# Sums of gathered lower rows for tiles 8 to 15 between the results of the down product

## The chip, the cores and the metric

The kernel runs on the eight cores of one Trainium2 chip, each with its own share of the rows and no traffic between them. The metric is the device time of the slowest core in microseconds, as the median of several runs.

## The reference

One layer: attention of 1024 wide rows with a causal mask, and then a mixture of eight experts with two chosen for each row, beside a shared expert. What matters here is the end of it:

```python
h = silu(einsum('nd,edf->nef', xf, w1))
ye = einsum('nef,efd->ned', h, w2)
routed = einsum('ne,ned->nd', combine, ye)          # two experts of eight for a row
shared = silu(gate) * up @ shared_down
shared = sigmoid(xf @ shared_gate_w) * shared
x = x + routed + shared
```

The output of a row is its own value after attention, plus two expert rows, each by its weight, plus the row of the shared expert by its gate.

## The kernel before

A core holds 16 tiles of 128 rows (NT = 16), each with its sum O[t] of 128 by 1024 floats in SBUF. After attention the rows are sorted by expert, 640 places for each (CAP). For each of the eight experts the loop `for ex in range(8)` computes the up product (L1089), the activation (L1096) and the down product (L1114) of five groups of 128 rows; a result is copied to one of three ys buffers, by VectorE (L1127) or, for expert 7, by ScalarE (L1124), and stored to Y in HBM by SyncE's queue (L1129).

Each row then needs two rows of Y: the lower of its two places (side 0, always of experts 0 to 6) and the higher one (side 1). `gather(t, side, ...)` has GpSimd issue one indirect DMA of 128 rows, 512 KB, for tile t into one of six buffers gb (L1150), with b = (side * NT + t) % 6. It waits until the buffer's last user is done (g_free[b]), and for the stores of Y that it needs: those up to expert 6 for side 0 (y_low), all for side 1 (y_free). `add_row` has VectorE add the gathered rows, times their weights, to O[t] (L1158), and records this as the buffer's release and as the new o_done[t].

The shared expert's down product (L1174) runs on TensorE for the 16 tiles in turn, 16 matmuls each, into two po buffers; VectorE adds each result to O[t] (L1181), which frees the po buffer and needs o_done[t]. Its weights are in SW1[0] (k_dw).

Every engine executes its own list of instructions in the order in which the program appended them, and a wait holds all that stands behind it. In the stretch in question that order is: VectorE takes the 16 adds of side 0, then for each t the result of tile t and the add of side 1 for tile t - 2. GpSimd issues the 16 gathers of side 0, then the 16 of side 1. SyncE stores a tile's output (L1187) after its second add. The adds of side 0 can begin while expert 7 is still computed.

```python
    g_free = [None] * 6
    ...
        b = (side * NT + t) % 6
```

Of the kernel before, what the change touches and what calls it, by code (L numbers as in the profile page):

```python
# [14 lines left out]
NT = 16  # L15
# [66 lines left out]
def build_program():  # L82
# [744 lines left out]
    while x < n_units or x <= max(retire_at):  # L827
        if x < n_units:
            kb, t = units[x]
# [318 lines left out]
    def gather(t, side, rows, *after):  # L1148
        b = (side * NT + t) % 6
        return b, SPOOL.dma(lambda e: e.indirect_dma_start(  # L1150
            out=gb[b][:], out_offset=None, in_=Y[0:rows, :],
            in_offset=bass.IndirectOffsetOnAxis(ap=lohi[:, side * NT + t:side * NT + t + 1], axis=0)),
            d_g[b], g_free[b], rows_out, *after)
# [3 lines left out]
    def add_row(t, side, b, k):  # L1157
        o_done[t] = SDVE.do(lambda e: e.scalar_tensor_tensor(  # L1158
            out=O[t][:], in0=gb[b][:], scalar=clh[:, side * NT + t:side * NT + t + 1], in1=O[t][:],
            op0=ALU.mult, op1=ALU.add), k, k_clh, o_done.get(t), ret[t]["xf"], o_back.get(t))  # L1160
        g_free[b] = o_done[t]

    for t in range(NT):
        b, k = gather(t, 0, 7 * CAP, *y_low, k_low, k_lohi)
        add_row(t, 0, b, k)
    SPE.wait(k_dw)
    for t in range(NT + 2):
        if t < NT:
            j = n % 2
            n += 1  # L1170
            SPE.wait(po_free[j], *[hb_ready[fc, t // 4] for fc in range(8)])
            for fc in range(8):
                for h in range(2):
                    fn = lambda e, fc=fc, h=h, j=j, t=t: e.matmul(  # L1174
                        po[j][:, h * 512:h * 512 + 512], HB[:, fc * 2048 + t * 128:fc * 2048 + t * 128 + 128],
                        SW1[0][:, fc * 1024 + h * 512:fc * 1024 + h * 512 + 512], start=(fc == 0), stop=(fc == 7))
                    if fc == 7 and h == 1:
                        k = SPE.do(fn)
                    else:
                        SPE.quiet(fn)  # L1180
            po_free[j] = o_done[t] = SDVE.do(lambda e, j=j, t=t: e.scalar_tensor_tensor(  # L1181
                out=O[t][:], in0=po[j][:], scalar=g_sb[:, t:t + 1], in1=O[t][:], op0=ALU.mult, op1=ALU.add),
                k, *cg_ready[t], o_done[t])
        if t >= 2:
            b, k = gather(t - 2, 1, 8 * CAP, *y_free)
            add_row(t - 2, 1, b, k)
            k_out = SSP.dma(lambda e, t=t - 2: e.dma_start(out=out[t * 128:(t + 1) * 128, :], in_=O[t][:]), d_outs,  # L1187
                            o_done[t - 2])
# [97 lines left out]
```

How the kernel before makes its waits and increments, by code:

```python
    def wait(self, *tokens):  # L38
        for t in tokens:
            if t is None:
                continue
            sem, val = t
            if val <= 0 or self.passed.get(id(sem), 0) >= val:
                continue
            self.passed[id(sem)] = val
            self.q.append(lambda e, s=sem, v=val: e.wait_ge(s, v))
# [1 line left out]
    def do(self, fn, *tokens):  # L48
        self.wait(*tokens)
        self.n += 1
        self.q.append(lambda e, f=fn, s=self.sem: f(e).then_inc(s, 1))
        return (self.sem, self.n)
# [5 lines left out]
    def dma(self, fn, slot, *tokens):  # L58
        self.wait(*tokens)
        slot.n += 16
        self.q.append(lambda e, f=fn, s=slot.sem: f(e).then_inc(s, 16))
        return (slot.sem, slot.n)
# [1128 lines left out]
    def run(e, main, one, other):  # L1191
        for fn in main.q:
            fn(e)
        full = e.alloc_register("full")
        e.wait_ge(*k_flag)
        e.reg_load(full, flag[0:1, 0:1])
        with e.If_eq(full, 0):
            for fn in one.q:
                fn(e)
        with e.Else():
            for fn in other.q:
                fn(e)
```

## Time and profile before

| | us |
|---|---|
| median of 3 runs | 1337.18 (1337.04 to 1341.15) |
| the profiled execution | 1337.72 |
| its span on the slowest core, 7 | 1336.2 |
| spans of the eight cores | 1319.4 to 1336.2 |
| TensorE busy, core 7 | 1145.8 (86%) |
| VectorE busy | 574.1 (43%) |
| ScalarE busy | 466.1 (35%) |
| GpSimd busy | 265.2 (20%) |

All is of one execution, taken on the slowest core unless another is named. Times in views count from the first instruction of that core. PE is TensorE, PEld its weight loads, DVE VectorE, ACT ScalarE, POOL GpSimd, SPq the queue of SyncE. A bracket behind a row of the timeline gives how long the engine stood idle before it and what released it. A row `x16` stands for several instructions merged. PEclk is the granted TensorE clock, where 1.00 is 2.4 GHz and 0.50 is 1.2 GHz. The landing of a DMA is the time from the start of its issue to its arrival.

### The profile page before, as it was taken

To read this page: it belongs to the slowest core of one execution; us is meant where nothing else is said; L and a number is where in the kernel's file an instruction comes from. 1 tells how busy PE (TensorE), PEld (TensorE's weight loads), DVE (VectorE), ACT (ScalarE), POOL (GpSimd) and SP (SyncE) were. 2 spreads that over 40 slices of the span, in tenths; PEclk is the share of its full clock that TensorE was granted. 3 is DMA by queue.
4 is the path that set the end of the run, shared out by engine and by line. 5 is a ranking of instruction groups with operands and counts; after the bars stand their busy time and mean duration, and the time that the engine had idled before them with its cause. 6 is when DMAs were issued, how large, how long until landed. Compare 5 with 4: busy or idle time off the path is not lost.

```text
span 1336.2 us, 18688 instructions; the slowest of 8 cores (1319.4 to 1336.2 us)
## 1 busy us (share of the span) xinstructions
PE 1145.8 (86%) x6280; PEld 580.3 (43%) x6280; DVE 574.1 (43%) x1273; ACT 466.1 (35%) x900; POOL 265.2 (20%) x435
## 2 busy tenths in 40 slices
PE   4678879778989898996978578699996999999887
PEld 1355445323434343442433233244563666666433
DVE  2354335335656665665674754312111111111466
ACT  2244233324543543644545443421321332222200
POOL 4101102111021112023121031360021222121431
PEclk9889889888989999998989879899998999999988
DMA  9936434997666766778959577599199999999977
GB/s 166 227 74 129 118 64 72 248 243 168 123 161 141 166 144 149 152 160 198 196 118 187 91 129 111 96 170 165 44 211 215 206 213 220 221 207 207 313 262 264
DMA packets 258828, 225.43 MB, mean 169 GB/s; under 512 B 197156, under 2 KB 203428, under 8 KB 258728
## 3 DMA queue, kind: packets, MB, share of 16 engines
q0 software_dynamic: 52848, 129.02, 45.4%
q1 hardware_dynamic: 205880, 95.14, 33.4%
q8 instruction: 54, 0.88, 0.3%
q14 instruction: 46, 0.38, 0.1%
HBM read 172.22 MB, written 51.38 MB: 167 GB/s over the span
## 4 chain that ended last, share of the span: by engine, by line
PE 53%; DMA 17%; DVE 12%; ACT 8%; issue 6%; SPq 3%; POOL 1%; DVEq 0%; ACTq 0%; POOLq 0%
PE po L605 11%; PE po L1114 8%; PE sp L1089 8%; PE sp L790 7%; PE sp L542 7%; DMA PT<-P 5%; PE po L1174 4%; PE po L484 4%; DVE per_unit L560 3%; DMA XT<-XN 3%; PE po L666 2%; DMA O<-xkv 2%; ACT P L572 2%; DMA Y<-ys 2%; DMA gb<-Y,lohi 2%
## 5 line engine op out<-in xcount | busy, mean ns | idle before, releaser
L605 PE MATMUL po<-XN,PT 128*128 128x512 bf16 x1088 | 259.3, 393 | 50.6 <-DMA PT<-P 40.8
L542 PE MATMUL sp<-XT,QT 128*128 128x512 bf16 x1088 | 255.0, 387 | 25.6 <-DMA XT<-XN 24.6
L605 PEld LDWEIGHTS po<-XN,PT 128*128 128x128 bf16 x1088 | 107.7, 101 | 193.3 <-issue 79.8
L542 PEld LDWEIGHTS sp<-XT,QT 128*128 128x128 bf16 x1088 | 106.2, 99 | 155.6 <-issue 38.2
L1127 DVE COPY ys<-po 128x1024 f32<-128x1024 f32 x35 | 42.9, 1224 | 229.8 <-PE po L1114 207.0
L790 PE MATMUL sp<-QT,WGU 128*128 128x512 bf16 x512 | 117.2, 390 | 5.9 <-DVE HB L805 5.5
L570 ACT ACTIVATE per_unit<-nm,s_q 128x1 f32<-128x1 f32 x72 | 21.2, 295 | 256.9 <-DVE nm L567 105.4
L618 DVE SCALAR_TENSOR_TENSOR O<-O,per_unit,po 128x512 f32<-128x512 f32 x112 | 80.5, 742 | 55.5 <-PE po L605 54.1
L484 PE MATMUL po<-XT,M 128*128 128x256 bf16 x512 | 65.3, 291 | 28.8 <-DMA XT<-XN 15.7
L1096 ACT ACTIVATE hT<-sp 128x640 bf16<-128x640 f32 x64 | 45.1, 704 | 113.4 <-PE sp L1089 113.4
L560 DVE TENSOR_REDUCE per_unit<-sp 128x1 f32<-128x1024 f32 (+1 forms) x72 | 83.4, 1158 | 1.6
L790 PEld LDWEIGHTS sp<-QT,WGU 128*128 128x128 bf16 x512 | 50.6, 100 | 68.8 <-issue 13.4
L572 ACT ACTIVATE P<-sp,per_unit 128x1024 bf16<-128x1024 f32 (+1 forms) x72 | 76.8, 1067 | 10.5
L69 POOL DMA_DIRECT2D xs<-xkv x60 | 32.5, 545 | 229.4 <-ACT XN L277 141.7
L666 PE MATMUL po<-WV,QT 128*128 128x512 bf16 x256 | 64.4, 397 | 10.8 <-DVE O L618 8.1
L1114 PE MATMUL po<-SW,hT 128*128 128x512 bf16 x320 | 73.2, 385 | 0.0
L1114 PE MATMUL po<-W,hT 128*128 128x512 bf16 x320 | 72.3, 379 | 0.0
L1089 PE MATMUL sp<-xt,W 128*128 128x320 bf16 x512 | 70.4, 299 | 1.5 <-ACT xt L926 1.5
L484 PEld LDWEIGHTS po<-XT,M 128*128 128x128 bf16 x512 | 52.6, 104 | 42.1 <-issue 32.0
L1089 PE MATMUL sp<-xt,SW 128*128 128x320 bf16 x512 | 70.2, 299 | 0.0
L69 POOL DMA_DIRECT2D O<-xkv x64 | 34.3, 548 | 168.4 <-ACT mvr L262 83.1
L1174 PE MATMUL po<-W,HB 128*128 128x512 bf16 x256 | 58.3, 392 | 10.6 <-DVE O L1181 10.6
(147 smaller groups left out, 1321.3 us busy)
## 6 DMA issues: line engine op xcount, KB each, us to landing
Y<-ys SPq DMA_DIRECT2D x40, 512.0 KB, 8.9
O<-xkv POOLq DMA_DIRECT2D x64, 256.0 KB, 5.7
xs<-xkv POOLq DMA_DIRECT2D x60, 256.0 KB, 3.9
G<-zero POOLq DMA_DIRECT2D x8, 1280.0 KB, 7.7
xn<-G SPq DMA_DIRECT2D x8, 1280.0 KB, 20.7
xr<-xkv POOLq DMA_DIRECT2D x16, 512.0 KB, 4.9
W<-w1p POOLq DMA_DIRECT2D x32, 256.0 KB, 16.4
W<-w2p POOLq DMA_DIRECT2D x32, 256.0 KB, 21.1
```

What stands on the lines that cost most here:

```text
L69: k = queue.dma(lambda e, i=i: e.dma_start(out=out[:, i * w:(i + 1) * w], in_=src[:, i * v:(i + 1) * v]), slot, *tokens)
L484: fn = lambda e, d1=d1, d2=d2, i=i: e.matmul(ring[i][:, 0:256], M[:, d1 * 1024 + d2 * 128:d1 * 1024 + d2 * 128 + 128], rhs(d1), start=(d1 ...
L542: fn = lambda e, d=d, h=h: e.matmul(sp[j][:, h * 512:h * 512 + 512], QT[:, d * 2048 + t * 128:d * 2048 + t * 128 + 128], XT[kb % 2][:, h * ...
L560: a = DVE.do(lambda e: e.reduce_max(lb[:, z:z + 1], sp[j][:, 0:n], axis=AX.X, negate=True), a)
L572: exp_tok[x] = ACT.do(lambda e: e.activation(out=P[p][:, 0:n], in_=sp[j][:, 0:n], func=AF.Exp, bias=ebias[:, z:z + 1], accum_out=lsum[:, z ...
L605: fn = lambda e, c=c, h=h, i=i: e.matmul(ring[i], PT[p][:, c * 128:c * 128 + 128], XN[kb % 2][:, c * 1024 + h * 512:c * 1024 + h * 512 + 5 ...
L618: ring_free[i] = DVE.do(lambda e, i=i, dst=dst: e.scalar_tensor_tensor(out=dst, in0=dst, scalar=corr[:, z:z + 1], in1=ring[i], op0=ALU.mul ...
L666: PE.quiet(lambda e, d=d, h=h, b=b: e.matmul(ring[b], QT[:, d * 2048 + t * 128:d * 2048 + t * 128 + 128], WV[:, d * 1024 + h * 512:d * 102 ...
L790: fn = lambda e, d=d, part=part: e.matmul(sp[j][:, part * 512:part * 512 + 512], WGU[fc][:, d * 256 + part * 128:d * 256 + part * 128 + 12 ...
L1089: fn = lambda e, d=d, h=h, fc=fc, i=i, j=j, xt_=xt_: e.matmul(sp[j][:, h * 512:h * 512 + H], SW1[i][:, d * 1024 + fc * 128:d * 1024 + fc * ...
L1114: fn = lambda e, fc=fc, h=h, s=s, i=i, j=j: e.matmul(po[j][:, h * 512:h * 512 + 512], hT[:, fc * CAP + s * 128:fc * CAP + s * 128 + 128], ...
L1174: fn = lambda e, fc=fc, h=h, j=j, t=t: e.matmul(po[j][:, h * 512:h * 512 + 512], HB[:, fc * 2048 + t * 128:fc * 2048 + t * 128 + 128], SW1 ...
```

## The change

The body of the first loop becomes a function `low_row(t)`, the gather of side 0 and its add. It is called for tiles 0 to 7 where the loop stood. For tiles 8 to 15 it is called in the loop of the down product, `low_row(8 + t)` ahead of the result of tile t. Both the gather on GpSimd and the add on VectorE are appended there.

```diff
--- before.py
+++ after.py
@@ -1160,11 +1160,17 @@
             op0=ALU.mult, op1=ALU.add), k, k_clh, o_done.get(t), ret[t]["xf"], o_back.get(t))
         g_free[b] = o_done[t]
 
-    for t in range(NT):
+
+    def low_row(t):
         b, k = gather(t, 0, 7 * CAP, *y_low, k_low, k_lohi)
         add_row(t, 0, b, k)
+
+    for t in range(8):
+        low_row(t)
     SPE.wait(k_dw)
     for t in range(NT + 2):
+        if 8 + t < NT:
+            low_row(8 + t)
         if t < NT:
             j = n % 2
             n += 1
```

## Rows read from the trace of the kernel before

**Rows 1.** The cores: span of each, and its mean granted TensorE clock.

```profile
core 7: 1336.2 us, clock 0.938
```

**Rows 2.** The chain of waits, core 7, 1240 to 1336 us: start, us, what.

```profile
1233.70 9.22 DMA gb<-Y,lohi
...
1243.16 1.30 DVE O L1158
...
1245.19 0.50 POOL gb L1150
...
1270.27 1.20 DVE O L1158
...
1275.24 0.14 issue
1275.38 51.29 PE po L1174 x224
```

**Rows 3.** The timeline of core 7: start, us, engine, line, operation [idle before <-releaser].

```profile
1257.67 7.07 PE L1174 MATMUL po<-W,HB 128*128 128x512 bf16 x32
...
1258.48 1.29 DVE L1158 SCALAR_TENSOR_TENSOR O<-gb,clh,O 128x1024 f32<-128x1024 f32 x1 [1.29 <-DMA gb<-Y,lohi]
...
1269.50 1.62 POOL L1150 DMA_INDIRECT gb<-Y,lohi  x1 [5.67 <-DMA Y<-ys]
...
1275.38 51.28 PE L1174 MATMUL po<-W,HB 128*128 128x512 bf16 x224 [10.64 <-DVE O L1181]
...
1281.94 1.28 DVE L1181 SCALAR_TENSOR_TENSOR O<-po,g_sb,O 128x1024 f32<-128x1024 f32 x1 [5.52 <-PE po L1174]
```

**Rows 4.** The waits of core 7, 1240 to 1336 us: us in total, times, longest.

```profile
POOL gb L1150 <- DVE O L1158: 37.7, 13, 7.9
```

**Rows 5.** Stretches of core 7: length, busy time by engine, PEclk, DMA share, GB/s.

```profile
1260.00:1265.00 5.00, 4.74 (x22) 1.96 (x20) 2.06 (x2) 0.00 (x0) 1.87 (x2) 1.00 0.96 318
...
1275.00:1282.00 7.00, 6.62 (x18) 2.49 (x19) 1.48 (x3) 0.00 (x0) 1.88 (x2) 0.57 0.97 343
1282.00:1290.00 8.00, 8.00 (x38) 3.63 (x37) 6.12 (x6) 0.00 (x0) 1.87 (x2) 1.00 0.47 151
```

**Rows 6.** Landings of gathers: core 5 all; core 7 from 1284; core 7 1255 to 1263.

```profile
DMA to landing us min/median/max: 4.7/6.7/12.8
...
DMA to landing us min/median/max: 5.8/6.6/7.1
...
L1150 POOL DMA_INDIRECT gb<-Y,lohi x5: 936/937/1686, 1253.4 to 1262.9; - x5
...
DMA to landing us min/median/max: 9.8/12.2/13.6
```

**Rows 7.** Timelines of core 3 (first three) and core 5 (last two): first lower gathers.

```profile
1218.38 1.00 POOL L1150 DMA_INDIRECT gb<-Y,lohi  x1 [22.43 <-PE sp L1089]
1219.65 0.98 POOL L1150 DMA_INDIRECT gb<-Y,lohi  x1 [0.27 <-issue]
...
1225.63 7.92 DVE L1158 SCALAR_TENSOR_TENSOR O<-gb,clh,O 128x1024 f32<-128x1024 f32 x6 [0.99 <-DMA gb<-Y,lohi]
...
1222.65 0.98 POOL L1150 DMA_INDIRECT gb<-Y,lohi  x1 [0.27 <-issue]
...
1229.07 7.58 DVE L1158 SCALAR_TENSOR_TENSOR O<-gb,clh,O 128x1024 f32<-128x1024 f32 x6 [1.50 <-DMA gb<-Y,lohi]
```

**Rows 8.** The timeline of core 0.

```profile
1237.91 2.97 PE L1114 MATMUL po<-SW,hT 128*128 128x512 bf16 x13
...
1244.93 0.70 ACT L1096 ACTIVATE hT<-sp 128x640 bf16<-128x640 f32 x1 [5.33 <-remote]
...
1245.78 17.16 PE L1114 MATMUL po<-SW,hT 128*128 128x512 bf16 x65 [4.90 <-ACT hT L1096]
...
1249.71 1.02 ACT L1124 ACTIVATE ys<-po 128x1024 f32<-128x1024 f32 x1 [4.08 <-remote]
...
1262.77 55.42 PE L1174 MATMUL po<-W,HB 128*128 128x512 bf16 x251
```

## The prediction

> **What bounds the kernel now.** First the spans of the eight cores [rows 1]: core 7 is the slowest, 1336.2 us, so its end is read first. Its chain of waits from 1240 us [rows 2] runs along gathers and VectorE adds until 1273.95 us, then on TensorE for 51.29 us without a break, and closes with VectorE's last adds. The reader is to see where TensorE entered that chain: it had begun the down product at 1257.67 us, did two tiles, and stood still until 1275.38 us [rows 3]. The second of those rows gives 10.64 us of idling, released by the VectorE step L1181. There are two po buffers, and VectorE had first to get through all 16 adds of lower rows, which were themselves waiting for gathers. After the stop the granted clock is 0.57 on average to 1282 us and then 1.00 [rows 5], that is 1.2 GHz almost to 1282 us. The first tile took from 1275.38 to its result's step at 1281.94 [rows 3], 6.5 us instead of 3.45 (16 tiles in 55.42 us on core 0 [rows 8]). So this stop costs core 7 10.6 + 3.1 = 13.7 us. Not every core has this stop: core 0 runs its 16 tiles through from 1262.77 us [rows 8]. The stop is what the change could remove. I ask what it puts there.
>
> **The change by parts.** No instruction is added or removed on any engine: still 32 gathers, 32 adds of 1.28 us, 16 results of 1.28 us, 16 stores. Eight adds move on VectorE, to before the results of down tiles 0 to 7. But the moved function also issues the gather, so eight gathers move on GpSimd too. GpSimd's order becomes: low 0 to 10, high 0, low 11, high 1, low 12, high 2, and so on to low 15, high 5, then high 6 to 15. There are six gb buffers: low t uses t mod 6, high t uses (t + 16) mod 6. Low 10 and high 0 share buffer 4; low 11 and high 1 buffer 5; 12 and 2 buffer 0; 13 and 3 buffer 1; 14 and 4 buffer 2; 15 and 5 buffer 3. These are exactly the gathers that now stand next to each other. High t can't be issued before the add of low t + 10 is over, and low t + 11 is queued behind it on GpSimd.
>
> **Start.** VectorE has low 0 to 8 behind it by about 1259.8 us (low 8's add starts at 1258.48 [rows 3]); these gathers keep their places. Tiles 0 and 1 end on TensorE at 1257.67 + 6.9 = 1264.6; the result of tile 1 goes first, low 10's add follows 1.20 us later (pitch of adds in a row [rows 2]) and ends at 1267.1. From an add's end to the issue that waits for it: 1243.16 + 1.30 to 1245.19 [rows 2], 0.75 us. So high 0 is issued at 1267.9. It also waits for expert 7's last Y store, which holds it until 1269.50 now [rows 3]; with five gathers fewer in flight I take the store to land sooner. Bounds: 0 to +1.6 us. The 10.6 us stop does vanish here: tiles 2 to 4 run to about 1275 us. Late next is GpSimd.
>
> **The loop, which is the price.** One turn, from the issue of high t to that of high t + 1: 1.27 us until low t + 11 is issued behind it (1219.65 less 1218.38 [rows 7]); that gather's landing, L; 0.24 us until VectorE starts (1233.70 + 9.22 against 1243.16 [rows 2]); the add, 1.28; 0.75 to the next issue. C = 3.5 + L. High t's own add and the down result fit into L, since high t lands earlier. For L the nearest rows are the second gathers of a burst on an idle queue: issue to add 1219.65 to 1225.63 and 1222.65 to 1229.07 us [rows 7], less 0.24, so 5.7 and 6.2 us. Below them is 4.7, the shortest landing on core 5; above them 7.1, the longest in the last stretch, where each gather runs beside a store [rows 6]. I take 6.0, as a turn too holds a store and two gathers: C = 9.5 us, between 8.2 and 10.6. TensorE needs 3.45 us a tile, or 6.5 at the low clock, so it waits in every turn. Five such turns lead from high 0 to high 5: 1267.9 + 47.5 = 1315.4 us.
>
> **After the loop.** High 5 lands and its add starts about 5.5 us after its issue (the shortest landings are 4.7 on core 5 and 5.8 in the last stretch of core 7 [rows 6], and 0.24 comes on top). The result of tile 8 stands behind it, starts 1.2 us later and takes 1.28; TensorE can then begin tile 10, 0.14 us on (as 1275.24 to 1275.38 [rows 2]): 8.1 us after the issue, at 1323.5. Tile 9 has run meanwhile, even at the low clock. Six tiles at 3.45: 1344.2. From TensorE's last matmul to the end of the span is 1336.2 - 1326.67 = 9.5 us now [rows 1, 2], and nothing in it changes: 1353.7 us. High gathers 6 to 10 follow high 5 every 1.24 us and hide under the tiles; if they didn't, their landing would cost 2 or 3 us once. For the clock after the last wait I take nothing, tile 9 having run just before; the bound is one tile's 3.1 us.
>
> **Which core.** The sum is P + 96.0, P being the start of the down product. P is 1257.67 on core 7 and 1262.77 on core 0 [rows 3, 8], so core 0 may now end last, at 1358.8. It is late because ScalarE stood twice, 5.33 and 4.08 us, on something outside the engines ("remote") while the gathers filled the queue [rows 8]. The first falls while low 0 to 10 are in flight, as they will be; the second might shrink with low 11 to 15 gone. With only the first, P is 1237.91 + 17.3 + 4.9 = 1260.1 [rows 8] and the end 1356.1. I take the slowest span as 1357. The profiled run took 1337.72 us for a span of 1336.2, and the median of the runs is 0.5 below it, so 1.0 is added: **1358 us**, 1.6% slower.
>
> The Trainium skill, "DMA: Bandwidth & Descriptors", section "Anatomy of one DMA — SWDGE (gpsimd) path", gives a GpSimd DMA about 2.0 us plus bytes over 436e3, an estimate of 3.2 us for one of these 512 KB. The trace disagrees: 4.7 us is the least [rows 6]. By that figure a turn would be bound by VectorE's two adds, the loop would lose some 14 us of its cost, and the kernel would end near 1340.
>
> **Rivals.**
> (a) Slower by the loop, as above. For it: the buffer numbers, and that GpSimd already waits 37.7 us for these adds in 13 waits [rows 4], each harmless today as its gather is wanted a few tiles later. Chance 0.78 within 1349 to 1370.
> (b) The loop, with congested landings. Between 1253 and 1263 us five gathers took 9.8 to 13.6 us [rows 6], at a DMA share of 0.96 and 318 GB/s from 1260 to 1265 us [rows 5]. At L = 9.8, C is 13.3: 1358 + 19 = 1377. Against it: a turn moves 1.5 MB in 9.5 us, some 160 GB/s. 0.07; another 0.05 for 1370 to 1375 (clock, a longer stall of ScalarE, the store's wait together).
> (c) Short landings, so that removal of the stop repays the loop. For the end at 1336.2 C must be about 6.0, L about 2.5 us; no gather read landed in under 4.7. Threshold and price are those of the loop. 0.03 for within 0.3% or near it, 0.02 for 1341 to 1349. This is where the figure of the page "DMA: Bandwidth & Descriptors" of the Trainium skill would lead.
> (d) Faster: the loop doesn't form, for instance as GpSimd's gathers stay ahead of VectorE by whole buffers. TensorE then runs 16 tiles from 1257.67, ends at 1312.9, and the kernel at 1323 (the 13.7 us back); it decides from a turn under 6.0 us on. The order of issues in the code speaks against it. 0.05.
> (e) The change does not do what it says, since low adds wait no less than before: this is a part of (a).
>
> **How the numbers follow.** Likeliest (a), 1358. Low: C = 8.5 takes off 5, core 7 alone last takes off 3: about 1350. High: C = 10.6 adds 5.5, the store's wait 1.6, the clock 3, core 0 in full 2: 1370. Range 1349 to 1370 leaves out 0.22 or less. About 0.3%, 4 us, is what a measurement of this kernel tells from no change. Slower 0.92, same 0.03, faster 0.05.
>
> **What would show it.** The order of gathers on GpSimd with single waits of several us on L1158 before high 1 to high 5, these five about 9.5 us apart; on TensorE L1174 no stop after tile 1, but one in each of tiles 5 to 9, the chain going through gb gathers and L1158; the granted clock low in that stretch; GpSimd's high 0 near 1268 us; TensorE's last matmul near 1344 us on core 7, and core 0 last or near it. The prediction is wrong if high gathers are issued without waiting for the neighbouring low add, if L is far from 6 us, or if TensorE goes through after tile 5.

## The result

The changed kernel takes 1357.83 us (median of 4 runs, 1351.7 to 1364.48), the kernel before on the same chip 1339.14 (4 runs). The ratio is 1.0139, with a 95% interval of 1.0103 to 1.0174: 1.4% slower. Some executions of every kernel here ran with a lower granted clock on the cores of one die and took longer; they are in none of the times and ratios of this document, and only the profiles of ring, ring_three, lag_three and the repeat are of such executions. The profiled execution of the changed kernel took 1351.7 us. Two of its cores, span and mean granted clock:

```profile
core 0: 1346.5 us, clock 0.936
...
core 5: 1350.1 us, clock 0.940
```

Core 5 is the slowest, so it is read. GpSimd's and VectorE's rows of its timeline (start, us, engine, line [idle before <-releaser]); L1158 is the add, L1150 the gather, L1187 the result of a down tile (L1181 before). Low t and high t are the gathers of side 0 and side 1 for tile t:

```profile
1266.03 1.28 DVE L1158 SCALAR_TENSOR_TENSOR O<-gb,clh,O 128x1024 f32<-128x1024 f32 x1
1268.23 0.94 POOL L1150 DMA_INDIRECT gb<-Y,lohi  x1 [21.16 <-DVE O L1158]
...
1269.44 0.93 POOL L1150 DMA_INDIRECT gb<-Y,lohi  x1 [0.27 <-issue]
1272.77 1.28 DVE L1158 SCALAR_TENSOR_TENSOR O<-gb,clh,O 128x1024 f32<-128x1024 f32 x1 [3.21 <-DMA gb<-Y,lohi]
...
1274.62 1.28 DVE L1158 SCALAR_TENSOR_TENSOR O<-gb,clh,O 128x1024 f32<-128x1024 f32 x1 [0.56 <-DMA gb<-Y,lohi]
1275.82 1.28 DVE L1187 SCALAR_TENSOR_TENSOR O<-po,g_sb,O 128x1024 f32<-128x1024 f32 x1
1276.97 0.94 POOL L1150 DMA_INDIRECT gb<-Y,lohi  x1 [6.60 <-issue]
...
1278.18 0.94 POOL L1150 DMA_INDIRECT gb<-Y,lohi  x1 [0.27 <-issue]
1281.36 1.28 DVE L1158 SCALAR_TENSOR_TENSOR O<-gb,clh,O 128x1024 f32<-128x1024 f32 x1 [4.26 <-DMA gb<-Y,lohi]
1283.42 1.28 DVE L1158 SCALAR_TENSOR_TENSOR O<-gb,clh,O 128x1024 f32<-128x1024 f32 x1 [0.77 <-DMA gb<-Y,lohi]
...
1285.45 0.94 POOL L1150 DMA_INDIRECT gb<-Y,lohi  x1 [6.33 <-DVE O L1158]
```

This is one turn and its beginning. Low 10's add (1266.03) ends at 1267.3, high 0 is issued at 1268.23, low 11 behind it at 1269.44. High 0's add runs at 1272.77, low 11's at 1274.62, and then high 1 can be issued: 1276.97. The next turn ends at 1285.45. In the kernel before, GpSimd waits at this place for a store [rows 3]. TensorE's rows of the same core:

```profile
1257.58 17.43 PE L1180 MATMUL po<-W,HB 128*128 128x512 bf16 x80
1277.25 3.61 PE L1180 MATMUL po<-W,HB 128*128 128x512 bf16 x16 [2.24 <-DVE O L1187]
1286.04 5.23 PE L1180 MATMUL po<-W,HB 128*128 128x512 bf16 x16 [5.18 <-DVE O L1187]
1294.42 3.61 PE L1180 MATMUL po<-W,HB 128*128 128x512 bf16 x16 [3.15 <-DVE O L1187]
1303.02 5.27 PE L1180 MATMUL po<-W,HB 128*128 128x512 bf16 x16 [4.99 <-DVE O L1187]
1312.03 5.30 PE L1180 MATMUL po<-W,HB 128*128 128x512 bf16 x16 [3.73 <-DVE O L1187]
1318.52 3.61 PE L1180 MATMUL po<-W,HB 128*128 128x512 bf16 x16 [1.19 <-DVE O L1187]
1322.59 17.43 PE L1180 MATMUL po<-W,HB 128*128 128x512 bf16 x80 [0.46 <-DVE O L1187]
```

The one stop of 10.64 us after tile 1 [rows 3] is gone, and there are six others, in front of tiles 5 to 10: 2.24 + 5.18 + 3.15 + 4.99 + 3.73 + 1.19, with a last one of 0.46 in front of tile 11: 20.9 us. The waits of core 5, 1255 to 1350 us (total, times, longest):

```profile
POOL gb L1150 <- DVE O L1158: 51.8, 8, 21.2
...
DVE O L1158 <- DMA gb<-Y,lohi: 29.3, 10, 5.3
PE po L1180 <- DVE O L1187: 20.9, 7, 5.2
```

And its chain of waits in the same stretch (start, us, what), with one landing for each turn:

```profile
1269.44 5.09 DMA gb<-Y,lohi
...
1274.62 1.30 DVE O L1158
...
1276.97 0.94 POOL gb L1150
...
1278.18 5.14 DMA gb<-Y,lohi
...
1286.66 5.04 DMA gb<-Y,lohi
...
1293.83 5.21 DMA gb<-Y,lohi
...
1302.43 5.61 DMA gb<-Y,lohi
...
1312.64 7.16 DMA gb<-Y,lohi
...
1322.59 17.44 PE po L1180 x80
```

GpSimd's 37.7 us of waits for adds [rows 4] have become 51.8, and now they lie in the chain: a gather, an add, GpSimd, the next gather. In three stretches (length, then busy time of TensorE, its weight loads, VectorE, ScalarE and GpSimd with their instructions, then PEclk, DMA share and GB/s):

```profile
1257.60:1275.00 17.40, 17.40 (x81) 7.70 (x79) 7.90 (x7) 1.02 (x1) 1.87 (x2) 1.00 0.27 94
1275.00:1318.50 43.50, 23.04 (x81) 8.64 (x81) 19.46 (x16) 0.00 (x0) 13.20 (x14) 0.88 0.56 186
1318.50:1340.00 21.50, 21.02 (x96) 9.24 (x96) 15.97 (x13) 0.00 (x0) 5.38 (x6) 1.00 1.01 367
```

In the middle one, 43.5 us, TensorE is busy for 23, VectorE for 19.5, GpSimd for 13 and the DMA engines for 56%. No engine fills it; what it waits for is each time the next issue.

**A measure that scatters less.** The start of the down product, P, lies between 1228 and 1258 us on the eight cores of this one execution. Most of that spread is older than the stretch in question: the last up matmul (L1089) ends between 1211 and 1238 us. So I read each core's span less its own P. "P less up" is the time from the end of the last up matmul to P. The granted clock from P to the last matmul was 0.85 to 1.00 on every core of every profile here, but for pool_only further down, where it was 0.78 or 0.79.

| profiled execution | span less P, eight cores | latest P | P less up |
|---|---|---|---|
| before | 65.0, 65.2, 72.7, 65.0, 75.4, 72.5, 77.8, 78.5 | 1262.8 | 24.9, 27.9, 17.1, 31.8, 17.1, 17.1, 17.1, 17.1 |
| after | 93.3, 95.0, 93.2, 94.0, 93.1, 92.5, 94.6, 92.5 | 1257.6 | 17.1 but for 19.2 (core 5) and 25.5 (core 7) |

The stretch became 14 to 30 us longer, but the kernel only 19. One reason is that the slowest core before, 7, had the longest stretch, 78.5, and lost the least. The other is in the last column: the cores that had 65 us and no stop of TensorE, 0, 1 and 3, are the three that came late to P, 25 to 32 us after the last up matmul instead of 17. While they were late their lower rows were added (all 16 adds are over by P), so the stop was saved at the price of a delay of 8 to 15 us. Counted from the end of the last up matmul (the two columns added), the kernel before takes 89.6 to 96.8 us, 92.8 at the median of the cores, and the changed one 110.2 to 118.0, 111.4 at the median: 18.6 us more, which is what the kernel lost.

### The profile page after: what moved, and what is told of

Same layout as the page of the kernel before. It is cut to its first block, busy times and chain, and to the rows that moved or that the text cites. A ratio compares the mean times of both kernels' runs of the same rounds, so it can differ in the third digit from the quotient of the medians.

```text
span 1350.1 us, 18678 instructions; the slowest of 8 cores (1323.2 to 1350.1 us)
## 1 busy us (share of the span) xinstructions
PE 1146.2 (85%) x6280; PEld 580.6 (43%) x6280; DVE 574.2 (43%) x1273; ACT 465.9 (35%) x900; POOL 264.1 (20%) x435
## 4 chain that ended last, share of the span: by engine, by line
PE 57%; DMA 17%; DVE 11%; ACT 6%; issue 5%; SPq 3%; POOL 0%; DVEq 0%; ACTq 0%; POOLq 0%
PE po L605 12%; PE po L1114 9%; PE sp L1089 9%; PE sp L542 8%; PE sp L790 7%; DMA PT<-P 5%; PE po L484 4%; PE po L666 3%; DMA XT<-XN 3%; DMA gb<-Y,lohi 2%; DVE per_unit L560 2%; DMA O<-xkv 2%; ACT P L572 2%; PE po L1180 2%; DMA Y<-ys 2%
## 5 line engine op out<-in xcount | busy, mean ns | idle before, releaser
L542 PE MATMUL sp<-XT,QT 128*128 128x512 bf16 x1088 | 252.2, 385 | 22.3 <-DMA XT<-XN 21.2
L570 ACT ACTIVATE per_unit<-nm,s_q 128x1 f32<-128x1 f32 x72 | 21.2, 295 | 257.7 <-DVE nm L567 101.4
L484 PE MATMUL po<-XT,M 128*128 128x256 bf16 x512 | 69.0, 302 | 32.6 <-DMA XT<-XN 19.5
L1096 ACT ACTIVATE hT<-sp 128x640 bf16<-128x640 f32 x64 | 44.9, 704 | 117.6 <-PE sp L1089 110.5
L1180 PE MATMUL po<-W,HB 128*128 128x512 bf16 x256 | 61.5, 402 | 20.9 <-DVE O L1187 20.9
L1089 PE MATMUL sp<-xt,W 128*128 128x320 bf16 x512 | 70.4, 299 | 1.5 <-ACT xt L926 1.5
L1089 PE MATMUL sp<-xt,SW 128*128 128x320 bf16 x512 | 70.2, 299 | 0.0
## 6 DMA issues: line engine op xcount, KB each, us to landing
W<-w1p POOLq DMA_DIRECT2D x32, 256.0 KB, 15.7
```

The lines of the kernel that those rows point to most:

```text
L484: fn = lambda e, d1=d1, d2=d2, i=i: e.matmul(ring[i][:, 0:256], M[:, d1 * 1024 + d2 * 128:d1 * 1024 + d2 * 128 + 128], rhs(d1), start=(d1 ...
L542: fn = lambda e, d=d, h=h: e.matmul(sp[j][:, h * 512:h * 512 + 512], QT[:, d * 2048 + t * 128:d * 2048 + t * 128 + 128], XT[kb % 2][:, h * ...
L1089: fn = lambda e, d=d, h=h, fc=fc, i=i, j=j, xt_=xt_: e.matmul(sp[j][:, h * 512:h * 512 + H], SW1[i][:, d * 1024 + fc * 128:d * 1024 + fc * ...
L1180: fn = lambda e, fc=fc, h=h, j=j, t=t: e.matmul(po[j][:, h * 512:h * 512 + 512], HB[:, fc * 2048 + t * 128:fc * 2048 + t * 128 + 128], SW1 ...
```

## The experiments

### VectorE's sequence alone, and GpSimd's alone

```diff
-        return b, SPOOL.dma(lambda e: e.indirect_dma_start(
+        (last if side else first).append(lambda: SPOOL.dma(lambda e: e.indirect_dma_start(
...
+    for issue in first + last:
+        issue()
```

The adds stay where the change puts them, the 16 lower gathers are issued first.

> One half of the change alone: VectorE's sequence as changed, but GpSimd issues all 16 lower gathers first, as in the kernel before. Queue theory (the loop forms because low t + 11 stands behind high t on GpSimd): the five turns vanish, the span less the start of the down product (P) falls from 92.5 to 95 us to about 66, and the median to 1323 to 1330 us. Buffer theory (high t and low t + 10 share a buffer, and VectorE's new order adds low t + 10 only just before high t is wanted): the turns stay, now of 0.75 (issue after the add) + about 4.8 (landing of a lone gather) + 0.24 + 1.2 (high's add) + 1.28 (next low add) = 8.3 us, between 8.0 and 8.8, so the median stays between 1350 and 1360 us.

Measured: ratio 1.0173 (1.0062 to 1.0283, from two executions); span less P 88.6 to 92.2 us on the eight cores. Core 0:

```profile
1257.93 0.94 POOL L1153 DMA_INDIRECT gb<-Y,lohi  x1 [2.70 <-DVE O L1162]
...
1262.52 2.48 DVE L1162 SCALAR_TENSOR_TENSOR O<-gb,clh,O 128x1024 f32<-128x1024 f32 x2 [3.26 <-DMA gb<-Y,lohi]
...
1265.75 0.94 POOL L1153 DMA_INDIRECT gb<-Y,lohi  x1 [6.88 <-DVE O L1162]
...
1271.10 2.48 DVE L1162 SCALAR_TENSOR_TENSOR O<-gb,clh,O 128x1024 f32<-128x1024 f32 x2 [4.91 <-DMA gb<-Y,lohi]
...
1274.33 0.94 POOL L1153 DMA_INDIRECT gb<-Y,lohi  x1 [7.65 <-DVE O L1162]
...
1281.81 0.94 POOL L1153 DMA_INDIRECT gb<-Y,lohi  x1 [6.55 <-DVE O L1162]
```

The lower gathers are all issued before the first high one (the last at 1254.29), and the turns are there all the same: 7.82, 8.58 and 7.48 us from one high gather to the next. High's add and the next low add now follow each other at once (x2), and the low one frees the buffer of the next high gather. The queue theory falls: at the median of the eight cores the stretch is only 3 us shorter than with the whole change (90.5 against 93.3). In the chain of this core these gathers, with no second one behind them, land in 4.09 to 5.19 us, against 5.04 to 5.61 in the changed kernel: a difference of the size of those 3 us.

The other half, with VectorE's 16 adds first:

```diff
-    for t in range(8):
+    for t in range(NT):
         low_row(t)
...
+    for issue in first[:11] + [f for i in range(5) for f in (last[i], first[11 + i])] + last[5:]:
+        issue()
```

> The other half alone: GpSimd's sequence as changed, VectorE's as in the kernel before. Both theories agree on a turn here: low 11 to 15 each wait behind a high gather that waits for the low add before it, 1.24 + about 5.2 + 0.24 + 1.28 + 0.75 = 8.7 us, five times, and nothing of the down product's results can be taken meanwhile: TensorE stops after tile 1 for about 40 us and the time is 1365 to 1378 us. If instead GpSimd's order costs nothing by itself, the time is that of the kernel before, 1337 to 1341.

Measured: 1377.57 us (one execution; the kernel before took 1344.2 there), span less P 108.3 to 111.2. Core 3, two of the turns and TensorE after them:

```profile
1281.45 0.94 POOL L1153 DMA_INDIRECT gb<-Y,lohi  x1 [6.69 <-issue]
1282.65 0.93 POOL L1153 DMA_INDIRECT gb<-Y,lohi  x1 [0.27 <-issue]
1287.90 1.28 DVE L1162 SCALAR_TENSOR_TENSOR O<-gb,clh,O 128x1024 f32<-128x1024 f32 x1 [7.52 <-DMA gb<-Y,lohi]
1289.94 0.94 POOL L1153 DMA_INDIRECT gb<-Y,lohi  x1 [6.35 <-DVE O L1162]
...
1315.72 14.57 PE L1182 MATMUL po<-W,HB 128*128 128x512 bf16 x56 [40.93 <-DVE O L1189]
```

A turn of 8.49 us, five of them in front of all results, and TensorE stops once, for 40.93 us. So each half makes the loop by itself, and the halves don't add: in the changed kernel they share the same round trip, and at the median of the cores the stretch is 93.3 us, beside 90.5 for VectorE's half and 109.6 for GpSimd's.

### The buffer numbers

```diff
-        b = (side * NT + t) % 6
+        b = gn[0] % 6
+        gn[0] += 1
```

> The changed kernel with the buffer of a gather numbered by the order of issue (a ring of six) in place of (16 * side + t) mod 6; the order on both engines is that of the change. Buffer theory: a gather waits for the add six places back, the turns vanish, TensorE has no stop but perhaps 1 to 3 us near tile 4 while high 0 waits for the last Y store; span less P 65 to 70 us, median 1322 to 1332, below the kernel before by about 1%. Rival, VectorE's load (three steps of 1.25 us a tile while low adds last, against 3.45 for TensorE): the turns shrink only to 3.75 and the gain is the same within 2 us, so this run can't tell a small load from none, but it would show any other cause by a stop of TensorE that stays at 8 us a tile and a median above 1350.

Measured: span less P 66.1 to 73.5 us. On core 5 TensorE runs its 16 tiles in 55.6 us without a stop:

```profile
1261.57 55.64 PE L1182 MATMUL po<-W,HB 128*128 128x512 bf16 x256
```

Both orders are those of the change; only the numbers differ, and 24 us of the stretch are gone at the median of the cores (69.5). This shows the buffer theory. The other seven cores kept stops, of 0.4 to 6.4 us in all. On core 7 they are 4.02, 0.34 and 1.10 us, and the gathers come late there: the add that starts at 1283.75 us is of a gather (low 12) issued at 1272.28, some 11 us earlier, in a stretch with a DMA share of 0.99. These are the long landings of rival (b), which the loop had kept away.

The time is another matter: ratio 0.9966 (0.9915 to 1.0017), a median of 1340.9 against 1344.2 on that chip. I had expected 1322 to 1332, and this failed. There was less to win than the 13.7 us of core 7: without its stop, core 0 with the latest P would have ended last, at 1327.8 in place of 1336.2. And counted from the last up matmul the ring takes 88.6 us at the median of the cores, only 4 less than the kernel before.

### One number changed: how many rows come first

```diff
-    for t in range(8):
+    for t in range(10):
...
-        if 8 + t < NT:
-            low_row(8 + t)
+        if 10 + t < NT:
+            low_row(10 + t)
```

> The changed kernel with one number changed: ten lower rows come ahead of the down product, not eight, so low t + 10 is added two tiles before high t is. Buffer numbers unchanged. Buffer theory: a gather needs about 0.75 + 5 + 0.24 + 1.28 = 7.3 us from the add that frees its buffer to the end of its own, which two tiles (6.9 us) and the slack of the two po buffers nearly cover: no turn over 3.8 us, span less P 66 to 70 us on cores whose gathers are early, a stop of 1 to 3 us after tile 1 on those whose are late; median 1322 to 1332. Queue theory expects the same order of size. If the loop came from neither (for instance from gathers and output stores sharing the DMA engines), about half of it would stay and the median would be above 1340.

> The changed kernel with nine lower rows ahead of the down product in place of eight. Buffer theory: low t + 10 is added one tile before high t is wanted, so a round trip (0.75 + about 5 + 0.24 + 1.28 for high t's add + 1.28 for the low add behind it = 8.5 us) is spread over two tiles: turns of 4.3 us against TensorE's 3.45, five of them; span less P about 70 us (69 to 73), between the 66.3 to 71.0 of ten ahead and the 92.5 to 95.0 of eight, and much nearer the former. A theory in which a turn's cost shrinks evenly with each row moved would give about 81.

Measured: with ten, span less P 66.3 to 71.0 us; with nine, 71.0 to 74.0. Two executions with ten took 1336.33 and 1343.44 us (the kernel before 1344.2 there; 1322 to 1332 was expected and not reached), one with nine 1338.0 (1337.3). On core 0 with nine:

```profile
1280.47 3.61 PE L1180 MATMUL po<-W,HB 128*128 128x512 bf16 x16 [0.30 <-DVE O L1187]
1287.52 33.18 PE L1180 MATMUL po<-W,HB 128*128 128x512 bf16 x144 [3.43 <-DVE O L1187]
```

The cost does not fall evenly with the rows moved: at the median of the cores the step from eight to nine takes away 21 us (93.3 to 72.6), the one to ten 4 more (68.7). The round trip spread over two tiles had given about 70.

### A seventh buffer

```diff
-gb = [... for i in range(6)]
+gb = [... for i in range(7)]
...
-        b = (side * NT + t) % 6
+        b = (side * NT + t) % 7
```

> The changed kernel with seven gather buffers in place of six and the numbers taken mod 7; order on both engines unchanged. Now high t shares its buffer with low t + 9, added one tile earlier than low t + 10: the same distance as with nine rows ahead, reached by another way. Buffer theory: span less P as there, 69 to 74 us. If the loop came from the order of the queues or from the transfers themselves, one more buffer would change little: 88 to 95.

Measured: span less P 74.0 to 78.0, time 1345.14 in one execution (1337.3 before). The same distance of one tile more, reached through the buffers, takes 18 us off (median 75.2). It stays 3 above nine rows (72.6), where I expected the same; with nine rows the lower row's own gather is also issued a tile earlier. That reason is argued, not shown.

### Later higher rows, and the hold of three

The ring left small stops. The next kernel takes higher rows from tile 4 on:

```diff
-        if t >= 2:
-            b, k = gather(t - 2, 1, 8 * CAP, *y_free)
+        for u in {10: [6, 7], 11: [8], 12: [9, 10], ...}.get(t, [t - 4] if t > 3 else []):
+            b, k = gather(u, 1, 8 * CAP, *y_free)
```

> Buffers numbered in order of issue, as in the ring, and the higher rows first taken at tile 4 in place of 2, with two in one tile at tiles 10 and 12, so that the end of the kernel is unchanged. It aims at the stops of 1 to 4 us that the ring left where high 0, held by the last Y store, is wanted. Theory: they go, TensorE runs its 16 tiles in 55.4 to 57 us, span less P 65 to 67 us on every core against 66.1 to 73.5 in the ring. If they came from the DMA queue being full rather than from the late start of high 0, stops of 1 to 3 us stay somewhere before tile 8. Time: the start P differs by up to 30 us between cores and runs, so the median can be 1325 to 1345; expected about 0.98 of the kernel before.

Measured: TensorE's 16 tiles in 55.4 to 58.0 us, as expected, but the tail from its last matmul to the end grew from 9.3 to 11.2 (ring) to 13.3 to 15.7, so span less P is 69.8 to 73.2 and not the expected 65 to 67. Core 7, the last third of the tiles and the tail (PEclk, DMA share and GB/s last):

```profile
1290.00:1308.00 18.00, 17.28 (x81) 7.64 (x78) 14.17 (x12) 0.00 (x0) 4.90 (x5) 1.00 1.00 333
1308.00:1322.00 14.00, 0.00 (x0) 0.00 (x0) 5.65 (x5) 0.00 (x0) 0.00 (x0) 0.57 0.76 290
```

The gain was given back in the tail. That the 16 gathers and 16 stores lack room there, at a DMA share of 1.00, is argued and not shown: in its last tiles the changed kernel had a share of 1.01 and a tail of 10.1. Ratio 0.9961 (0.9917 to 1.0004), where I had expected 0.98.

The same with at most three lower gathers in flight while expert 7 runs:

```diff
+        held = adds[gn[0] - 4] if 4 <= gn[0] <= 11 else None
...
-            d_g[b], g_free[b], rows_out, *after)
+            d_g[b], g_free[b], rows_out, held, *after)
```

> The same, and the fourth to eleventh lower gather each also wait for the add of the gather three places before, so that no more than three are in flight while expert 7 is computed. It tests what makes P late on single cores: ScalarE stops marked remote of 2 to 19 us, seen only while five or six gathers are in flight. If a queue full of gathers holds something that ScalarE needs, they go and the down product starts 17.1 us after the last up matmul on all cores; the time falls by some 3 to 8 us against late_high. If they have another cause, they stay in two to four cores of eight. Price of the hold, if any: later lower rows, a stop after tile 1 of up to 5 us.

Measured: P less up is 17.1 us on all eight cores, against 22.6 and 21.2 on cores 7 and 5 without the hold. ScalarE's waits marked remote, which stood on cores 5, 6 and 7, are on no core. The waits of core 7 without the hold, 1220 to 1262 us:

```profile
ACT hT L1096 <- remote: 9.1, 2, 6.8
...
ACT ys L1124 <- remote: 3.9, 1, 3.9
```

With it, ScalarE's only waits in that stretch:

```profile
ACT ys L1124 <- PE po L1114: 12.5, 5, 2.8
ACT hT L1096 <- PE sp L1089: 4.4, 3, 1.6
```

Ratio 0.995 (0.9912 to 0.9989), a median of 1332.2 us against 1337.3: the only version here whose interval lies below the kernel before, by half a per cent, and one among several that were tried. Against the kernel without the hold (1333.2) no gain is shown, where I had expected 3 to 8 us. Two more versions in search of both: the same hold on the ring kernel, whose higher rows start at tile 2, and the hold with higher rows from tile 3:

```diff
-        for u in {10: [6, 7], 11: [8], 12: [9, 10], ...}.get(t, [t - 4] if t > 3 else []):
+        for u in ([t - 3] if 3 <= t < 9 else [6, 7] if t == 9 else [t - 2] if t > 9 else []):
```

> The ring (higher rows from tile 2 on) with the hold of three gathers in flight. The late start of the higher rows had taken TensorE's stops away (55.4 to 58.0 us for 16 tiles) but moved 16 gathers and 16 stores into a shorter time, and the tail from the last matmul to the end grew from 9.6 to between 13 and 16 us. If the two add up as they should, this one has 1 to 5 us of stops and a tail of 9.5 to 11: span less P 66 to 72 us; with the start of the down product 17.1 us after the last up matmul on every core. Ratio to the kernel before 0.985 to 0.995.

> The same, but the higher rows from tile 3 on, with two at tile 9. Between the two others: stops of 0 to 2 us, and as the catching up is early, a tail of 9.5 to 12: span less P 66 to 69 us. If the transfers themselves bound this stretch (16 higher gathers, 16 stores and the lower rows' rest, some 19 MB), it is no better than the ring and ends at 69 to 71 like the late start. Ratio to the kernel before 0.98 to 0.995.

Measured: 1.0014 (0.9964 to 1.0063) and 1.0009 (0.9954 to 1.0064), span less P 71.3 to 76.2 and 67.4 to 73.3. P less up is 17.1 on all 16 cores, as expected, but the ratios and the stretches of 66 to 72 and 66 to 69 us that I expected are not there. On the ring the hold lengthened TensorE's 16 tiles from 59 to 63 us at the median of the cores; the lower rows come later with it.

The hold alone on the kernel before, whose buffer numbers are those of the order of issue already:

```diff
-            d_g[b], g_free[b], rows_out, *after)
+            d_g[b], g_free[b], rows_out, held, *after)
```

> The kernel before with the hold alone. The remote stops of ScalarE go here too and the down product starts 17.1 us after the last up matmul on all cores. But those cores then have TensorE's stop after tile 1, as VectorE is not yet through with its 16 adds: span less P 72 to 80 us on all cores. The gain of the one is the loss of the other and the median stays within 5 us of the kernel before. If the hold were what gained in the others, it would gain here too, 5 us or more.

Measured: ratio 1.0146 (1.0033 to 1.0259), span less P 78.1 to 82.2, P less up 17.1 on all cores. Core 0:

```profile
1266.10 49.88 PE L1182 MATMUL po<-W,HB 128*128 128x512 bf16 x224 [10.44 <-DVE O L1189]
```

The stop on every core was expected, its size was not: all eight cores have the stop after tile 1 now, 10.4 to 15.4 us, longer than the 4.7 to 10.6 of the kernel before. I had expected a median within 5 us of the kernel before, and the ratio is above that. Counted from the last up matmul the hold takes 97.2 us at the median of the cores, 4.4 more than the kernel before. So the early start of the down product is worth nothing while all 16 lower adds stand in front of it. With eight of them moved away (late_high and three) the hold costs nothing, but that it gains anything in time is not shown by any pair here.

### The change once more

The same kernel, nothing edited, on another chip.

> The changed kernel once more, to size what the first profile can't: how much of the time is the stretch from the start of the down product (P) on, and how much is P itself. If the stretch is fixed by the round trip between VectorE and the gathers, span less P is 92 to 96 us on all eight cores and a turn 8.4 to 9.0 us, whatever the chip. P is then what scatters: the latest P of eight cores, 1257.6 in the first profile, should be 1255 to 1275, the spans of the slowest core 1348 to 1368, and the ratio to the kernel before 1.010 to 1.022. If instead the stretch itself scatters (span less P from 88 to 105 between cores), the round trip is not what sets it.

Measured: ratio 1.0112 (1.007 to 1.0153), span less P 91.6 to 95.6 us, five turns of core 0 in 43.4 us, 8.68 each, and 8.4 to 9.1 on the eight cores. The latest P was 1276.75 us. The slowest core's span was 1346.2 to 1361.0 us in six executions. The stretch is the same on another chip (93.5 us at the median of the cores, against 93.3), while P differed by 29 us between the cores of the first profile and by 38 in this one. So it is mainly P that moves the time.

## Why the prediction was right

The range and the sign held, and 1358 met 1357.83. That closeness is partly luck, as the terms show. They were made against one execution's spans, so they stand beside the profiled execution of the changed kernel, core 5:

| term | forecast | measured |
|---|---|---|
| P to the issue of high 0 | 10.2 | 10.65 |
| L, landing of the low gather in a turn | 6.0 | 5.0 to 5.6 |
| a turn, mean of five | 9.5 | 8.64 |
| five turns | 47.5 | 43.2 |
| issue of high 5 to TensorE's restart | 8.1 | 7.1 |
| from there to the last matmul | 20.7 | 21.5 |
| tail | 9.5 | 10.1 |
| span less P | 96.0 | 92.5 |

- **The loop and its place**: right. High 0 to high 5, five turns, tiles 5 to 9 among those that wait, TensorE through tiles 0 to 4 without a stop, and the stop of [rows 3] gone.
- **Start**: right to 0.5 us. The last Y store was not what held high 0: the row at 1268.23 names the add. From low 10's add, which ends at 1267.31, to that issue are 0.92 us, where 0.75 was taken.
- **L, the term that was mis-sized**: I took 6.0 from the second gathers of bursts of six [rows 7]. In the chain the landings are 5.09, 5.14, 5.04, then 5.21 and 5.61 for high gathers where those came last. A burst has up to four more gathers in flight; a turn has two and a store, at a DMA share of 56%. That is 0.86 us a turn, 4.3 us in all.
- **The estimate of 3.2 us**: the figure that the Trainium skill's page "DMA: Bandwidth & Descriptors" would give (section "Anatomy of one DMA — SWDGE (gpsimd) path") is not borne out in the turns: 5.04 is the least in the chain, and 4.2 the shortest on the five cores of the changed kernel whose views give one. Landings here count from the start of the issue, whose instruction alone takes 0.94 us on GpSimd. The recorded "near 1340" for this case doesn't follow from its own sum: 1358 less 14 is 1344. And the two adds would not have bound such a turn, since VectorE's three steps are 3.75 us and a turn of 3.5 + 3.2 is 6.7.
- **What the turn consists of**: half right. The text laid it to the queue, with high t's add hidden under L. In the chain the low gather came last in three turns by 0.5 to 0.8 us, and in two the high gather did. With GpSimd's order undone (the first experiment) the stretch is only 3 us shorter. The binding part is that a high gather waits for an add that VectorE does just before it wants the high row.
- **After the loop**: 1 us shorter to TensorE's restart, and 0.8 longer from there. High 6, issued at 1312.64, landed only after 7.16 us and stands in the chain, with TensorE's last stop of 0.46 us; the forecast had it hidden.
- **Which core**: failed. I had core 0 late by half of its ScalarE stops and the slowest span at 1357; it was 1350.1, on core 5, with P at 1257.58. The profiled execution (1351.7) was also the fastest of the four, and the median lies 6 us above it, where I had subtracted 0.5. The sum was 7 us above the execution it was made for, and the scatter between executions put back as much.
- **The clock**: as forecast, no tile was slow after the last wait (PEclk 1.00 from 1318.5 us), and in the turns it was lower, 0.88, with three tiles at 5.2 to 5.3 us in place of 3.6. They ran while the turn's gathers were under way.
- **Rival (d)**, gathers that stay ahead of VectorE by whole buffers, was badly put. With the gathers ahead in GpSimd's order little is gained; with the buffers ahead (the ring) most of the stops go; and even so the kernel isn't at 1323, since the cores without a stop had nothing to lose and most cores kept some.
- **Rival (b)** didn't occur in the changed kernel. Rival (c)'s short landings didn't either: at 5.0 they are far from 2.5.

## What to carry to other kernels

A buffer number computed from the tile is right for one order of issue only. When an operation is moved, write out for each buffer who uses it before and after, and count the steps between the add that frees it and the add that wants it again: here a round trip of 8.5 us stood against 3.45 us a tile, and both in the same tile cost 28 us over the 65 of an unbroken stretch, one tile apart 7 to 10, two apart 4. When several cores differ, a stop on one of them is worth only what it is above the next slowest core. And when a stretch is measured from its own start, look at what made the start late: the same delay may have hidden the stop.

## What was not expected of the hardware

ScalarE stood for 2 to 17 us at a time, at waits that the trace calls remote, with its input ready, while lower gathers (512 KB each) were issued as fast as buffers came free (DMA share 0.91 to 1.00 around such waits on two cores read); it is on two to four cores of eight in each of the ten profiles without the hold, and with at most three in flight on none of the 32 cores of four kernels. A full share alone is not enough: core 5 of the kernel before had 0.96 to 1.03 from 1230 to 1250 us and no such wait. What ScalarE waited for is not shown. In the code the copies (L1124) also wait for the store of their ys buffer, but the activations (L1096) only for TensorE. And the landing of a gather is 5.0 to 5.6 us in a turn at 186 GB/s, 4.09 to 5.19 for the high gathers of vec_only's core 0, but 9.8 to 13.6 at 318 [rows 5, 6].
